# Three key parts in memory, maxima ahead of operand loads, a leaner beginning and values in whole blocks, in a gated cross-attention kernel on Trainium2

## The chip, the cores and the metric

One core of a Trainium2 chip runs the kernel. It has five engines with their own instruction streams: TensorE (PE, matmuls and transposes into PSUM), ScalarE (ACT, activations), VectorE (DVE, reductions and elementwise work), GpSimd (POOL, elementwise work in SBUF) and SyncE (SP, which issues the transfers). They are ordered only by semaphores. The metric is the device time of one execution in microseconds (us).

## The reference

A batch of 16 sequences of 256 tokens with 128 features attends to 16 contexts of up to 1601 rows, with 16 heads of depth 8, and then passes through a mixture of 8 small experts. All in float32; the softmax runs over all 1601 keys.

```python
# attention: q from layernorm(x), k and v from ctx_1024
qh, kh, vh = split(layernorm(x) @ wq.T + bq), split(ctx @ wk.T + bk), split(ctx @ wv.T + bv)
attn = softmax(einsum('bhqd,bhkd->bhqk', qh, kh) / sqrt(8), axis=-1)
x = x + tanh(g_xattn[0]) * (einsum('bhqk,bhkd->bhqd', attn, vh) @ dense_w.T + dense_b)
# experts, on layernorm(x): sigmoid gates, the two best of 8, their weights normalised
h = gelu(x_n @ W1[e] + b1[e]);  y[e] = h @ W2[e] + b2[e]
x = x + tanh(g_ffn[0]) * (sum_e gate[e] * y[e] + gelu(x_n @ Ws1 + bs1) @ Ws2 + bs2)
```

## The kernel before

The 16 heads are 8 pairs of heads. One step `s` handles one batch `b = s // 2` and one half of its pairs (`GP = 4`), for all 256 queries and all 1601 keys, in 13 tiles of up to 128 keys; there are 32 steps. Four steps are one phase cycle, called a pass below: `PLAN` has one string for each step of it.

Scores are computed with the float32 operands split into three bfloat16 parts. A contraction over 48 rows holds six products of parts (`KPART`, `QPART`), each for the 8 features of a head; the two heads of a pair lie on two sides of the partitions (`SIDE`). Keys are split by `split_run` (DVE, batch 0) or `split_keys` (POOL, the others, four operations), stored to memory by `store_keys` (line 389) and loaded in the operand's layout by `load_operands` (line 318). `PLACES` says which parts are repeated: the first part of the keys stands in three places of the contraction, the second in two, the third in one. In the kernel before all six places are written to memory: `k_dram` has six slots, stored by three DMAs for each of two halves.

The softmax subtracts a maximum per query and head. `row_scores` (PE, line 741, called a row score below) computes scores of 128 queries against 512 keys for both heads of a pair, `maximum` (DVE, line 901) reduces them; 24 such and 2 for the rest of 65 keys make one step. `neg_max` is transposed on PE (unit `T`, line 697), copied by ACT (605), split in three by POOL (`split_maxima`), and `move_maxima` (SP, line 410) writes the parts to `m_dram` (416) and reads them back as three more rows of the query operand (419). So the score matmul already gives score minus maximum.

`score_pair` (PE, line 757, a pair below) computes keys against queries for four units in two of the three PSUM banks `a_ps`; ACT takes the exponential of each bank (573) into `probs`. `values` (PE, line 775) multiplies the probabilities of a tile of 128 keys with the values, four matmuls side by side in the array, summed in `o_ps`. A block is one such tile of one step; it can be done whole (512 columns, letter pair `VV` in `PLAN`) or in two halves of 256 columns (two `V` apart). The same three banks also serve, in order, the key projection of the next batches (`K`, line 688), the value projection (`V`, 692), the transposes of maxima and the second layer's tiles. Row scores, the dense projection and the second layer's outputs use two other slots, `b_ps`.

PE works in the order that `order(s)` writes out from `PLAN`: `P` a pair, `S` a row score (for the step after next or next), `V` values, `k` and `v` projections, `T` the transpose of the maxima of the next step, `d` the dense projection, `q` and `f` the query tiles and the second layer, `y` and `c` its output. `S` runs ahead of `P`: in step `s` the row scores of step `s + 1` are completed before `T`, and ten of step `s + 2` follow. ACT and DVE follow the same order for their parts.

SP issues all transfers in one stream. In step `s` it takes, in this order: outputs of the last step (`move_outputs`), in odd steps the keys two batches on (`store_keys`), the operands of step `s + 3` (`load_operands`), the reciprocal sums and the gates, in odd steps the two contexts (`load_context`), the maxima of step `s + 1` (`move_maxima`), the queries of the next chunk and the result. Each call first waits for what it needs, and all behind it wait too. Before step 0 SP loads the first context, weights, constants, all tokens and the value context, stores the first keys and queries, and loads the first operands.

## Time and profile before

| | us |
|---|---|
| time, median of 3 runs | 1434.74 (1431.17 to 1438.01) |
| the profiled execution | 1436.73 |
| its span, from the first to the last instruction | 1434.9 |
| PE busy | 1241.7 (87%) |
| ACT busy | 1055.6 (74%) |
| DVE busy | 1049.3 (73%) |
| POOL busy | 418.7 (29%) |
| mean granted clock of TensorE | 0.902 of full speed |
| bytes moved by DMA | 147.13 MB |

Busy time is the sum of an engine's instructions. A matmul that runs beside another counts in the same busy time, and a busy PE need not be at its peak: at a granted clock of 0.5 (1.2 GHz) the same matmuls are busy for longer than at 1.0 (2.4 GHz). A time in square brackets in a timeline row is the idle time of the engine just before, and the arrow names what ended it.

### The profile page before, as it was taken

To read this page: it belongs to the slowest core of one execution; us is meant where nothing else is said; L and a number is where in the kernel's file an instruction comes from. 1 tells how busy PE (TensorE), PEld (TensorE's weight loads), DVE (VectorE), ACT (ScalarE), POOL (GpSimd) and SP (SyncE) were. 2 spreads that over 40 slices of the span, in tenths; PEclk is the share of its full clock that TensorE was granted. 3 is DMA by queue.
4 is the path that set the end of the run, shared out by engine and by line. 5 is a ranking of instruction groups with operands and counts; after the bars stand their busy time and mean duration, and the time that the engine had idled before them with its cause. 6 is when DMAs were issued, how large, how long until landed. Compare 5 with 4: busy or idle time off the path is not lost.

```text
span 1434.9 us, 29778 instructions
## 1 busy us (share of the span) xinstructions
PE 1241.7 (87%) x11555; PEld 458.9 (32%) x11555; DVE 1049.3 (73%) x1208; ACT 1055.6 (74%) x1962; POOL 418.7 (29%) x309
## 2 busy tenths in 40 slices
PE   2448889798989999899989999799979999799855
PEld 1112323232323433243323333243323433243224
DVE  8477778587768888688868878688768868689001
ACT  1008879587978799688968789688968889689741
POOL 7242224051333215151424125051423205010111
PEclk6568999798988999899989999899989999899786
DMA  7673634636273653737273744637173744501101
GB/s 213 114 149 69 150 70 98 140 84 129 53 164 70 139 119 87 147 81 149 52 169 61 170 87 99 139 82 146 47 167 67 165 92 96 102 11 33 31 14 45
DMA packets 71390, 147.13 MB, mean 103 GB/s; under 512 B 13705, under 2 KB 37970, under 8 KB 71250
## 3 DMA queue, kind: packets, MB, share of 16 engines
q1 hardware_dynamic: 71250, 145.24, 47.4%
q8 instruction: 91, 1.49, 0.5%
q14 instruction: 49, 0.40, 0.1%
HBM read 88.30 MB, written 56.91 MB: 101 GB/s over the span
## 4 chain that ended last, share of the span: by engine, by line
PE 66%; DMA 14%; ACT 5%; DVE 4%; SPq 4%; POOL 3%; issue 2%; POOLq 0%; ACTq 0%; DVEq 0%
PE o_ps L775 26%; PE a_ps L757 15%; PE b_ps L741 11%; DMA m_dram<-nm_parts 10%; PE a_ps L688 4%; PE a_ps L692 4%; ACT probs L573 3%; PE b_ps L720 2%; DVE run_max L901 2%; SPq L406 2%; DMA q_op<-m_dram 1%; SPq L397 1%; PE a_ps L684 1%; PE b_ps L723 1%; DMA q_op<-q_dram 1%
## 5 line engine op out<-in xcount | busy, mean ns | idle before, releaser
L901 DVE TENSOR_REDUCE run_max<-b_ps 128x2 f32<-128x1024 f32 x768 | 899.4, 1218 | 249.4 <-PE b_ps L741 246.0
L573 ACT ACTIVATE probs<-a_ps 128x512 f32<-128x512 f32 (+1 forms) x1664 | 901.9, 594 | 144.3 <-PE a_ps L757 127.4
L775 PE MATMUL o_ps<-probs,v_op 128*32 128x256 f32 (+3 forms) x4928 | 505.8, 483 | 2.3 <-ACT probs L573 1.2
L757 PE MATMUL a_ps<-q_op,k_op 51*128 51x256 bf16 (+1 forms) x3328 | 338.1, 283 | 46.4 <-DMA q_op<-m_dram 25.6
L741 PE MATMUL b_ps<-k_op,q_op 48*128 48x512 bf16 (+1 forms) x2048 | 325.6, 350 | 37.5 <-DVE run_max L901 24.2
L757 PEld LDWEIGHTS a_ps<-q_op,k_op 51*128 51x128 bf16 (+1 forms) x3328 | 112.9, 97 | 373.5 <-ACT probs L573 307.3
L741 PEld LDWEIGHTS b_ps<-k_op,q_op 48*128 48x128 bf16 x2048 | 88.7, 96 | 208.2 <-DVE run_max L901 95.9
L775 PEld LDWEIGHTS o_ps<-probs,v_op 128*32 128x32 f32 (+1 forms) x4928 | 98.4, 109 | 176.4 <-issue 93.8
L509 POOL TENSOR_TENSOR attn<-num,den_all 128x256 f32<-128x256 f32 x16 | 11.6, 728 | 440.3 <-DMA den_all<-r_dram 440.3
L688 PE MATMUL a_ps<-kctx,wk_s 128*128 128x400 f32 (+1 forms) x128 | 81.4, 734 | 55.7 <-DMA kctx<-ctx_t 49.9
L469 POOL TENSOR_TENSOR nm_parts<-nm_t,one 8x256 bf16<-8x256 f32 x32 | 19.3, 602 | 360.5 <-ACT nm_t L605 360.5
L594 ACT ACTIVATE k_t<-a_ps,bk_s 128x401 f32<-128x401 f32 (+1 forms) x64 | 38.1, 597 | 106.7 <-PE a_ps L688 106.6
L692 PE MATMUL a_ps<-wv_s,vctx 128*128 128x128 f32 (+1 forms) x416 | 64.4, 294 | 0.0
L888 DVE SCALAR_TENSOR_TENSOR y_s<-b_ps,tgf,x_s 128x128 f32<-128x128 f32 x32 | 11.2, 349 | 71.3 <-PE b_ps L724 71.2
L599 ACT ACTIVATE v_op<-a_ps 128x512 f32<-128x512 f32 x64 | 32.9, 513 | 36.7 <-PE a_ps L692 36.3
L692 PEld LDWEIGHTS a_ps<-wv_s,vctx 128*128 128x128 f32 (+1 forms) x416 | 51.2, 192 | 20.8 <-issue 11.5
L469 POOL TENSOR_TENSOR k_parts<-k_t,one 128x1601 bf16<-128x1601 f32 x15 | 42.8, 2850 | 43.8 <-ACT k_t L594 43.8
L688 PEld LDWEIGHTS a_ps<-kctx,wk_s 128*128 128x128 f32 x128 | 25.9, 248 | 83.1 <-issue 61.0
L904 DVE TENSOR_REDUCE run_max<-b_ps 128x8 f32<-128x520 f32 x64 | 43.9, 696 | 10.3 <-PE b_ps L741 10.3
L471 POOL TENSOR_TENSOR k_t<-k_t,k_parts 128x1601 f32<-128x1601 f32 x15 | 48.5, 3230 | 1.2
L475 POOL TENSOR_TENSOR k_parts<-k_t,k_parts 128x1601 bf16<-128x1601 f32 x15 | 45.3, 3021 | 1.2
L473 POOL TENSOR_TENSOR k_parts<-k_t,one 128x1601 bf16<-128x1601 f32 x15 | 42.8, 2851 | 1.2
(100 smaller groups left out, 680.4 us busy)
## 6 DMA issues: line engine op xcount, KB each, us to landing
k_op<-k_dram SPq DMA_DIRECT2D x64, 600.4 KB, 9.5
k_dram<-k_parts SPq DMA_DIRECT2D x32, 600.4 KB, 6.0
kctx<-ctx_t SPq DMA_DIRECT2D x16, 800.5 KB, 12.5
vctx<-ctx_t SPq DMA_DIRECT2D x16, 800.5 KB, 11.8
k_dram<-k_parts SPq DMA_DIRECT2D x32, 400.2 KB, 7.0
o_dram<-o_s SPq DMA_DIRECT2D x32, 256.0 KB, 2.1
g_all<-g_dram SPq DMA_DIRECT2D x16, 512.0 KB, 6.4
k_dram<-k_parts SPq DMA_DIRECT2D x32, 200.1 KB, 6.7
```

What stands on the lines that cost most here:

```text
L469: pool.tensor_tensor(parts[0], whole, ones(whole, slice(0, whole.shape[0])), ALU.mult).then_inc(chain, 1)
L471: pool.tensor_tensor(whole, whole, parts[0], ALU.subtract).then_inc(chain, 1)
L473: pool.tensor_tensor(parts[1], whole, ones(whole, slice(0, whole.shape[0])), ALU.mult).then_inc(chain, 1)
L475: pool.tensor_tensor(parts[2], whole, parts[1], ALU.subtract).then_inc(chain, 1)
L573: act.activation(probs[0:keys, unit % PB, :], a_ps[at % AB][0:keys, :], ACT.Exp, scale=SCALE).then_inc(a_taken, 1)
L688: last = pe.matmul(bank[:, 0:n_keys], wk_s[:, :], kctx[:, k0:k0 + n_keys], start=True, stop=True)
L692: last = pe.matmul(bank[0:KEYS[t], 128 * (t % 4):128 * (t % 4) + 128], vctx[:, 128 * t:128 * t + KEYS[t]], wv_s[:, :], start=True, stop=True)
L741: last = pe.matmul(slot[:, side, to:to + n_keys], q_op[buf][rows, p, 128 * t:128 * t + 128], k_op[buf][rows, p, k0:k0 + n_keys], start=Tru ...
L757: last = pe.matmul(a_ps[(at + side) % AB][0:KEYS[t], SEQ * a:SEQ * a + SEQ], k_op[buf][rows, slot, 128 * t:128 * t + KEYS[t]], q_op[buf][r ...
L775: last = pe.matmul(o_ps[32 * j:32 * j + 32, cols], v_op[s // 2 % 2][0:KEYS[t], t, GP * (s % 2) + j, :], probs[0:KEYS[t], unit % PB, cols], ...
L901: dve.tensor_reduce(run_max[:, t, :, p, c:c + 1].rearrange("q v o -> q (v o)"), slot[:, :, :], AX.X, ALU.max).then_inc(b_taken, 1)
L904: dve.tensor_reduce(run_max[:, i - FULL, :, :, RUNS], slot[:, :, 0:GP * REST].rearrange("q v (p k) -> q v p k", p=GP), AX.X, ALU.max).then ...
```

## The change

- **Three key parts.** `k_dram` holds each of the three parts once. `store_keys` issues two DMAs instead of six; `load_operands` issues three for the key operand of each side instead of one, each reading the first parts from memory again, so 8 DMAs a step instead of 4.
- **Order of SP.** In odd steps `move_maxima(s + 1)` stands ahead of `load_operands(s + 3)` and of the value context. The key context of batch `b + 3` is loaded in the even step, after the maxima, not in the odd one.
- **The beginning.** The first operands are loaded right after the first keys are stored; the queries of chunk 0 are stored from ACT's queue; only the tokens of chunk 0 are loaded ahead of them, those of chunk 1, the operands of step 1, the value context and the other tokens behind. DVE waits for the tokens where it first needs them. `first_maxima` reorders steps -2 and -1: five row scores before the key tiles, and all row scores and the transpose of step 0 ahead of the rest.
- **PLAN.** Four new strings. They hold the same numbers of `P`, `S`, `V`, `k`, `T`, `f`, `q` and `d`; every `V` now stands beside another, so that all blocks are whole. The four outputs of a chunk (`y`, `c`) are all in the second string.

```diff
-OP_DMAS = 4
+OP_DMAS = 2 * (len(PLACES) + 1)
-PART_STORES = 2 * len(PLACES)
+PART_STORES = 2
 PLAN = (
-    "SkSPVVPSkSPSkSPVVPSVPSVPSVPSVPSVPSVPSVPVSPyPSVVSPcSPVVPSSTkSPVVPSVPSVPSVPSVPdSPVVPVVPS",
-    "vSPSVVSPvSPVVSPyPcSPVVPSVVSPyPSfcPSVVPSfSPVVSPVVSPyPcSPVVSPSvPVVPSSTvVPSVPSVPSVPSVPVSPSVPVS",
-    "PVPSVPSkVPVSPSVPVPSVPSVPSfSPVVPSkSPVVPSVPSVPSVPSVSPVSPVSPSVVPSffffTfSPSVVvSPSkSPVVPSkSPVVP",
-    "dSPvSPSVVSPvSPVVPSVPSVPSVPSvVPSVPSVPSVPSVPSVPSVPSqSSPVVPqSPVVTPSVPSVPSVPSVPSVPSVPSVVP",
+    "PSkSPVVSPSvPSVVPSSPVVPSSPVVPkSSPVVPSkSPVVPSSPVVPSSPVVPSSPVVTSPSVVPdPSSPVVPVVPSkSPVVPS",
+    "yPcSPVVSSPvSPVVPSSPVVPSSPVVPSvSPSVVPVVSPyPcSPVVPSVVvPSSfSPVVPSTyPcSPVVSPSVVPyPcSPVVSPSVVPSfS",
+    "PSPVVPkSPVVPVVPkSPSkPVVPSSPVVPSfSPVVPSSPVVPSSPVVPSSPVVPSSPVVTPSSPVVPSkSPVVSPSfffffSSPVVS",
+    "vSPVVPSvSPSvPVVPSSPVVPSqSPVVPSSPVVPSSPVVPSSPVVPVVPdPSSvSPVVTSPSqPSVVPSSPVVPSSPVVPSSPVV",
 )
+def first_maxima():
+
+    scores = [event for event in ORDER[-2] if event[0] == "S"]
+    rest = [event for event in ORDER[-2] if event[0] != "S"]
+    first = [event for event in ORDER[-1] if event[0] == "S" and event[1] < SUNITS]
+    turn = [("A", ("T", 0, 0))]
+    return scores[:5] + rest + scores[5:], first + turn + [e for e in ORDER[-1] if e not in first + turn]
+
+
+ORDER[-2], ORDER[-1] = first_maxima()
...
-                    sp.dma_start(k_op[buf][rows, :, :].rearrange("r (a p) c -> r a p c", a=2),
-                                 kd[:, :, pairs, :]).then_inc(op_in[buf], 16)
+                    for r0, r1 in PLACES:
+                        to = slice(SIDE * side + DH * r0, SIDE * side + DH * r1)
+                        sp.dma_start(k_op[buf][to, :, :].rearrange("r (a p) c -> r a p c", a=2),
+                                     kd[0:DH * (r1 - r0), :, pairs, :]).then_inc(op_in[buf], 16)
...
-                    for r0, r1 in PLACES:
-                        sp.dma_start(k_dram[b % 2, a, r0:r1].rearrange("n r c -> r n c"),
-                                     k_parts[64 * a:64 * a + 64, 0:r1 - r0, :]).then_inc(k_written, 16)
+                    sp.dma_start(k_dram[b % 2, a].rearrange("n r c -> r n c"),
+                                 k_parts[64 * a:64 * a + 64, :, :]).then_inc(k_written, 16)
...
+            store_keys(0)
+            load_operands(0)
+            load_context("K", kctx, 1, kctx_in)
+            load_tokens(1, 2, x_in[1])
+            load_operands(1)
             load(vctx, ctx_t[0]).then_inc(vctx_in, 16)
-            store_keys(0)
-            load_context("K", kctx, 1, kctx_in)
-            store_queries(0)
-            load_operands(0)
+            load_tokens(2, CHUNKS, x_in[2])
             for s in range(FIRST, LAST + 1):
                 b = s // 2
                 if 0 <= s - 1 < STEPS:
                     move_outputs(s - 1)
                 if s % 2 == 1 and b + 2 < BATCH:
                     store_keys(b + 2)
-                if 0 <= s + 3 < STEPS:
+                if s % 2 == 0 and 2 <= s + 3 < STEPS:
                     load_operands(s + 3)
                 if s % 2 == 0 and 0 <= b - 1 < BATCH:
                     spread_sums(b - 1)
                 if s % 4 == 2 and 0 <= (s - 6) // 4 < CHUNKS:
                     spread_gates((s - 6) // 4)
-                if s % 2 == 1 and b + 3 < BATCH:
+                if 0 <= s + 1 < STEPS:
+                    move_maxima(s + 1)
+                if s % 2 == 1 and 2 <= s + 3 < STEPS:
+                    load_operands(s + 3)
+                if s % 2 == 0 and b + 3 < BATCH:
                     load_context("K", kctx, b + 3, kctx_in)
                 if s % 2 == 1 and 0 <= b + 2 < BATCH:
                     load_context("V", vctx, b + 2, vctx_in)
-                if 0 <= s + 1 < STEPS:
-                    move_maxima(s + 1)
...
# ACT, after the first units:
+            store_queries(act, 0)
# DVE, before statistics("q", (s + 6) // 4):
+                            if s < 4:
+                                dve.wait_ge(x_in[s // 4 + 2], 16 if s < 0 else 16 * (CHUNKS - 2))
```

## Rows read from the trace of the kernel before

**Rows 1.** Windows: stretch, length, busy (instructions) of PE, PEld, DVE, ACT, POOL, clock, DMA share, GB/s
```profile
426.00:587.30 161.30, 153.74 (x1448) 56.92 (x1446) 129.19 (x148) 132.09 (x246) 51.71 (x38) 0.93 0.52 112
```
**Rows 2.** Waits of PE, 110 to 1378 us: total, times, longest
```profile
PE a_ps L688 <- DMA kctx<-ctx_t: 36.7, 6, 7.7
PE a_ps L757 <- DMA q_op<-m_dram: 25.6, 15, 7.2
```
**Rows 3.** Timeline, 571 to 598 us: start, duration, engine, line, operation
```profile
571.86 0.33 SPq L332 DMA_DIRECT2D k_op<-k_dram  x1
...
575.44 0.29 SPq L416 DMA_DIRECT2D m_dram<-nm_parts  x1
...
585.35 1.68 PE L688 MATMUL a_ps<-kctx,wk_s 128*128 128x401 f32 x2 [4.40 <-DMA kctx<-ctx_t]
...
587.33 0.58 SPq L419 DMA_DIRECT2D q_op<-m_dram  x2
...
589.13 0.61 PE L757 MATMUL a_ps<-q_op,k_op 51*128 51x256 bf16 x4 [1.57 <-DMA q_op<-m_dram]
...
597.43 0.38 PE L757 MATMUL a_ps<-q_op,k_op 51*128 51x256 bf16 x4
```
**Rows 4.** Windows: the beginning, a wait, a lesser dip, a stretch without row scores
```profile
0.00:54.00 54.00, 12.04 (x21) 5.21 (x21) 29.73 (x34) 6.21 (x11) 25.85 (x17) 0.63 0.81 197
...
587.00:599.00 12.00, 10.43 (x53) 2.72 (x52) 6.04 (x5) 6.60 (x12) 0.00 (x0) 0.57 0.35 90
...
1146.80:1185.50 38.70, 36.24 (x319) 12.13 (x320) 25.63 (x25) 31.96 (x57) 3.26 (x5) 0.91 0.43 86
...
1355.00:1366.00 11.00, 9.35 (x116) 2.62 (x116) 0.00 (x0) 10.71 (x21) 0.00 (x0) 1.00 0.01 5
```
**Rows 5.** Timeline: maxima with an empty queue, and pairs with a whole block
```profile
137.06 0.27 SPq L416 DMA_DIRECT2D m_dram<-nm_parts  x1
138.43 0.56 SPq L419 DMA_DIRECT2D q_op<-m_dram  x2
...
1367.07 0.39 PE L757 MATMUL a_ps<-q_op,k_op 51*128 51x256 bf16 x4
...
1368.15 0.39 PE L757 MATMUL a_ps<-q_op,k_op 51*128 51x256 bf16 x4 [0.69 <-ACT probs L573]
...
1368.47 1.06 PE L775 MATMUL o_ps<-probs,v_op 128*32 128x512 f32 x8
...
1369.47 0.39 PE L757 MATMUL a_ps<-q_op,k_op 51*128 51x256 bf16 x4
...
1369.90 7.56 ACT L573 ACTIVATE probs<-a_ps 128x512 f32<-128x512 f32 x14 [0.23 <-PE a_ps L757]
```
**Rows 6.** Timeline: a key tile, and pairs with half blocks
```profile
65.78 0.94 PE L688 MATMUL a_ps<-kctx,wk_s 128*128 128x400 f32 x2
...
572.75 8.01 DVE L901 TENSOR_REDUCE run_max<-b_ps 128x2 f32<-128x1024 f32 x7 [0.84 <-PE b_ps L741]
...
573.21 0.39 PE L757 MATMUL a_ps<-q_op,k_op 51*128 51x256 bf16 x4
573.44 0.38 PE L741 MATMUL b_ps<-k_op,q_op 48*128 48x512 bf16 x2
...
574.32 0.39 PE L757 MATMUL a_ps<-q_op,k_op 51*128 51x256 bf16 x4
```
**Rows 7.** Timeline and chain of waits, the beginning
```profile
32.60 8.12 SPq L406 DMA_DIRECT2D q_dram<-q_parts  x12
54.16 1.03 PE L741 MATMUL b_ps<-k_op,q_op 48*128 48x512 bf16 x4 [12.48 <-DMA q_op<-q_dram]
...
96.17 12.79 DMA m_dram<-nm_parts
...
110.81 0.61 PE L757 MATMUL a_ps<-q_op,k_op 51*128 51x256 bf16 x4 [1.52 <-DMA q_op<-m_dram]
```
**Rows 8.** Key stores: issue time in ns, min/median/max
```profile
L397 SPq DMA_DIRECT2D k_dram<-k_parts x96: 581/1384/2912, 21.0 to 1208.9; - x96
```
**Rows 9.** Value matmuls by shape (eight to a block or half block)
```profile
L775 PE MATMUL o_ps<-probs,v_op 128*32 128x256 f32 x3072 | 250.5, 398 | 0.9 <-ACT o_s L581 0.4
```

More of the change, by code:

```diff
@@ L264, in flamingo_block @@
         y_s = sb("y_s", [128, 4, 128])
-        key_in, first_in, const_in, x0_in, x_in, ones_set = (sem(n) for n in ("key_in", "first_in", "const_in", "x0_in",
-                                                                              "x_in", "ones_set"))
+        key_in, first_in, const_in, ones_set = (sem(n) for n in ("key_in", "first_in", "const_in", "ones_set"))
+        x_in = [sem(f"x_in{i}") for i in range(3)]
         k_ones, v_ones = [sem(f"k_ones{i}") for i in range(4)], sem("v_ones")
@@ L297, in keys_split, with store_queries @@
                 engine.wait_ge(k_chain, 4 * b)
+        def store_queries(engine, c):
+            engine.wait_ge(q_chain, 4 * (c + 1))
+            for a in range(2):
+                for part, (r0, r1) in enumerate(PLACES):
+                    for r in range(r0, r1):
+                        engine.dma_start(q_dram[2 * c:2 * c + 2, a, r].rearrange("b r q -> r b q"),
+                                         q_parts[64 * a:64 * a + 64, part, :]
+                                         .rearrange("p (b q) -> p b q", b=2)).then_inc(q_written, 16)
         block = ctx.enter_context(nc.Block())
@@ L309, in _, with load_tokens @@
                 load(dst, src).then_inc(key_in, 16)
-            sp.dma_start(x_s[:, 0:4, :], x[:, 0:4, :]).then_inc(x0_in, 16)
+            def load_tokens(c0, c1, arrived):
+                for c in range(c0, c1):
+                    sp.dma_start(x_s[:, 4 * c:4 * c + 4, :], x[:, 4 * c:4 * c + 4, :]).then_inc(arrived, 16)
+            load_tokens(0, 1, x_in[0])
             for dst, src in firsts:
@@ L314, in _ @@
                 load(dst, src).then_inc(const_in, 16)
-            for c in range(1, CHUNKS):
-                sp.dma_start(x_s[:, 4 * c:4 * c + 4, :], x[:, 4 * c:4 * c + 4, :]).then_inc(x_in, 16)
             def load_operands(s):
@@ L395, in store_keys @@
                 for a in range(2):
-                    for r0, r1 in PLACES:
-                        sp.dma_start(k_dram[b % 2, a, r0:r1].rearrange("n r c -> r n c"),
-                                     k_parts[64 * a:64 * a + 64, 0:r1 - r0, :]).then_inc(k_written, 16)
-            def store_queries(c):
-                sp.wait_ge(q_chain, 4 * (c + 1))
-                for a in range(2):
-                    for part, (r0, r1) in enumerate(PLACES):
-                        for r in range(r0, r1):
-                            sp.dma_start(q_dram[2 * c:2 * c + 2, a, r].rearrange("b r q -> r b q"),
-                                         q_parts[64 * a:64 * a + 64, part, :]
-                                         .rearrange("p (b q) -> p b q", b=2)).then_inc(q_written, 16)
+                    sp.dma_start(k_dram[b % 2, a].rearrange("n r c -> r n c"),
+                                 k_parts[64 * a:64 * a + 64, :, :]).then_inc(k_written, 16)
             def move_maxima(s):
@@ L442, in _ @@
                     load_context("V", vctx, b + 2, vctx_in)
-                if 0 <= s + 1 < STEPS:
-                    move_maxima(s + 1)
                 if s % 4 == 3 and 0 < (s + 5) // 4 < CHUNKS:
-                    store_queries((s + 5) // 4)
+                    store_queries(sp, (s + 5) // 4)
                 if s % 4 == 1 and 0 <= (s - 9) // 4 < CHUNKS:
@@ L934, in _ @@
             dve.memset(k_op[0][:, :, :], 1.0).then_inc(k_ones[0], 1)
-            dve.wait_ge(x0_in, 16)
+            dve.wait_ge(x_in[0], 16)
             statistics("q", 0)
```

4 lines of the change are left out of this document (2 added, 2 removed).

## Prediction

> **What bounds the kernel now.** After the page's busy shares I read windows of four steps each. Such a pass (two batches of keys, one chunk of the second layer) is the unit that repeats; the five in the middle take 158 to 164 us, 162 in the mean, of which TensorE (PE) is busy 154, ScalarE (ACT) 132, VectorE (DVE) 129 in the one shown [rows 1]: three engines near each other, none full. Next, who waits: between the first score tile and the last, PE stands 36.7 us for a context transfer in 6 places and 25.6 us for the maxima rows in 15 [rows 2]. The reader is to see in the SyncE (SP) timeline how one place comes about: SP queues the operands of a later step, then two contexts, and only then the maxima of the next step; that tiny write, issued at 575.44, is followed by its dependent issue at 587.33, and the context for the keys lands so late that PE waits 4.40 us, then 1.57 us more [rows 3]. The granted clock is 0.57 in the 12 us around it and 1.00 in a stretch without such a wait [rows 4]; between 589.13 and 597.43 the matmuls run at 1.2 GHz. And the start: the first score tile runs at 110.81 us [rows 7].
>
> The profiled execution took 1436.73 us (span 1434.9), 2.0 above the median of the runs, 1434.74. I take differences from the trace and subtract them from the median.
>
> **Part 1, key parts and issues.** Per batch the stores fall from six DMAs (12 parts of 64 x 1601 x 2 bytes, 2401 KB) to two (6 parts, 1201 KB); their issue, 1.38 us each at the median [rows 8], falls from 8.3 to 2.8 us. The operand loads carry the same bytes in eight instead of four DMAs, each under 0.5 us of SP [rows 3]: under +2 us per step. Both lie beside compute; SP's next need in an odd step is the maxima, some 10 us later. Cost 0, bounds -1 to +2 us per step pair only if SP were late, which nothing in [rows 3] suggests after the reorder.
>
> **Part 2, maxima and contexts.** In odd steps the maxima go ahead of the next operand load and the value context; the key context moves to the step before and so lands some 30 us early. With nothing ahead of it the write takes 1.4 us from issue to dependent issue [rows 5] instead of 11.9. Gone: 36.7 us, and 24 of the 25.6 (1.5 belongs to the beginning), 61 together. With them goes what the low clock costs. From 589.13 to 597.43 PE did three score pairs, one whole value block, four row scores and two key tiles; at full clock a pair takes PE 0.31, a block 1.00, a row score 0.23, a key tile 0.94 [rows 5, 6]; that is 4.7 us, not 8.3, and the key tile before it took 0.7 more than it would: 4.3 us a place. Seven places (six contexts, one maxima wait of 7.2 us): 30. Five lesser dips in the second halves of passes, as one with a mean clock of 0.91 over 38.7 us [rows 4]: some 7 us at 1.2 GHz each, 35 together, 0.4 us lost per us as above, less the waits in them: 8. Sum -99, bounds -61 (clock falls for other reasons) to -110.
>
> What is queued behind the moved step matters. Behind the maxima now stand eight operand DMAs and then the value context. In the last step of a pass the new order puts the transpose of the maxima some eight score pairs before the end, and the next batch's first value tile after only three pairs of the new pass (before: late in the step before or at leisure). From the transpose: 0.7 us to ACT's end, 2.6 us of POOL (four splits of 0.60 to 0.66), write and rows, then eight issues: the context is issued about 9.3 us later. The queue moved 2994 KB from 571.86 to 587.33 [rows 3], 193 KB/us; 1393 + 800 KB from 5.7 us on end at 17.2. PE asks at 4 x 2.40 + 0.6 + 4 = 14.5. **New wait: 2.7 us**, eight times: +21. Bounds: 0 (if PE arrives later) to 5 us and a low clock, (5 + 4.3) x 8 = +74.
>
> **Part 3, values in whole blocks.** Before, 3072/8 = 384 half blocks and 216 whole ones [rows 9]; after, by counting the letters of the order, 416 whole. Halves run pair, row score, half, in 1.11 us, with no idle on PE; DVE needs 8.01/7 = 1.144, so two cost 2.29 [rows 6]. A whole block takes 1.00 on PE against 2 x 0.57 (1.11 less a pair and a row score, 0.54), but it stands between score pairs: 1367.07 to 1369.47 is pair, pair, block in 2.40 us, and ACT idles 0.23 in it [rows 5]. The three banks hold only one pair ahead. So a bare block costs 0.11 more; where another tile is in it, the 0.32 us that PE has free pays for it. Per pass, new: 52 x 2.40 = 124.8, plus what the tiles add beyond the slack (keys 8 x 0.55, values 4.8, second-layer outputs 4 x 1.2, hidden tiles with two table loads 6.5, all others 3.7) = 149.0. Old: 25 x 2.29 + 27 x 2.08 (two pairs, two row scores, a block) + the same tiles at full PE time 34.2 (keys 7.5, values 7.3, outputs 6.1, hidden 6.5, others 6.8) = 147.6; the traced pass less its stalls, 162 - 99/8 = 149.6, agrees within 2. **+1.4 a pass, +11 in all.** Bounds: PE's chain alone, 104 x 0.54 + 52 + 34.2 = 142.4 a pass (-42), and no slack used, 124.8 + 34.2 = 159 (+91); I take the value between, being the one that reproduces the old pass. In the last 36 pairs there are no row scores; ACT paces halves at 7.56/7 = 1.08 a pair [rows 5], blocks at 1.20: +4.
>
> **Part 4, the beginning.** Before: six key stores, key context, twelve query stores from 32.60 for 8.12 us, operands, first row scores 54.16 [rows 7]. The DMA engines are 0.81 busy at 197 GB/s [rows 4]: bytes, not latencies. After: nothing but constants ahead, stores 1.2 MB from 21, query stores on ACT beside them (0.8 MB from 21.9 on; twelve issues at SP's 0.68 end at 30.1), landed by 32.3; 1.4 MB of operands, issued in 3.4 us, landed near 43. The maxima of step 0 then take 26 x 1.14, statistics 1.4 and a wait of up to 2 for the second token chunk: 75. Before, the transpose waited behind the query tiles and the write took 12.79 us [rows 7]; now the rows are there at about 82. The ten row scores of step 1 (11.4 us of DVE) still stand ahead of the first pair, so it runs at 86, not 110.8. **-25**, bounds -12 (only the transfer chain shortens) to -32. The later token chunks, 1.5 MB, now share the queue with steps -1 and 0; their wait (before step 2) is 40 us away.
>
> One rule of the Trainium skill bears on this ("DMA: Bandwidth & Descriptors", section "Issuing engines are not separate DMA queues"): moving the query stores to ACT saves issue time only, as all queues share the same 16 engines. Had I granted the move no more than issue time, the start would gain the 8 us of issues and little from overlap, and the sum would stand some 5 us higher.
>
> **Sum**: 1434.7 - 25 - 99 + 21 + 11 + 4 = **1347 us**. The tail (57 us after the last pair) I cost at nothing: its output tiles fill the same wait for normalisation.
>
> **Rivals.**
> A. *PE-bound whole blocks.* The saved 0.14 us a block counts in full wherever other tiles lie and PE is the one without idle, as in the half-block stretch of [rows 6]. At 142.4 a pass, 6.6 less than I take: 1347 - 53 = 1294. Against: the 2.40 is measured.
> B. *The value context becomes the new place that drops the clock.* 5 us and 4.3 us eight times instead of 2.7: +53, 1400. For: same queue, same 2.2 MB as now. Against: maxima waits of 1 to 3 us in the middle left the windows at 1.00.
> C. *The beginning or the low clock gives little back* (ACT's stores slow, clock falls anyway): 1347 + 25 = 1372 or more.
> D. *Slower than before.* The new order sets two row scores side by side ahead of a pair. There are two slots in memory for them and DVE takes 1.14 us each, 2.29 of every 2.40; with its gates, statistics and divisions DVE is saturated, and a row score that waits holds the in-order PE and so the pair and ACT. The second is due 0.45 us after the first pair, which leaves 0.4 us until the banks would hold the pair anyway; from a wait of 0.61 us a block on (0.21 lost x 416 = 88) the gains are gone; at 0.7 us the time is 1347 + 125 = 1472. For: seven maxima in a row run without a gap now [rows 6]. Against: DVE is busy 129 of 161 us [rows 1], 129 of about 153 after.
> E. *The clock.* With 0.3 us idle in each block the clock could fall often. The rows speak against it: 1355 to 1366, pairs and halves alone with PE 85% busy, was granted 1.00 [rows 4], and pair, pair, block ran at its speed [rows 5]. A quarter of the steady stretch at 1.2 GHz would cost 0.4 x 300 = 120: 1467.
> The Trainium skill has that as a rule ("TensorE: Matmul & The Clock Gate", section "A second HAM failure mode: psum-queue depth-cycling"): short idles between groups of matmuls can make the clock oscillate. By that rule, E's 1467; the rows of this trace speak against it.
>
> **Chances.** Forecast 0.49 (its own range 1318 to 1375), A 0.17, B 0.13, C 0.11, D 0.06, E 0.04. Range for 8 in 10: 1295 to 1405, which takes in A's middle and B's. A measurement of this kernel tells 0.5% (7 us) from no change. Faster 0.87, same 0.04, slower 0.09: D and E almost whole, B and C with bad luck both.
>
> **What would show it.** First score tile near 86 us, first row scores near 43. No PE wait on the key context after it; maxima waits under 3 us in all; write to dependent issue about 1.4 us in odd steps. A wait of value tiles for their context, once a pass, under 4 us. Granted clock above 0.95 in the steady windows. 3328 value matmuls, block to block 2.40 us where nothing else is in it, a pass near 153 us. I am wrong if a pass is above 159 or below 145, or if ACT's idle for score tiles grows beyond DVE's.

## The result and the profile after

The changed kernel takes 1476.67 us (median of four, 1470.38 to 1490.08), the kernel before 1432.95 beside it (1426.57 to 1438.01): 1.032 times the time, 95% interval 1.024 to 1.040. It is slower by some 44 us where 88 less were forecast; 1477 lies outside the range. The profiled execution took 1470.38 us, its span is 1468.6. Below, medians are of all executions of a kernel and ratios of the undisturbed ones; the one execution of e4 that was traced took 2629.38 us against 1447 to 1456 of its three others, and nothing is read from it.

First the waits of PE, by line, tile and releaser (total, times, longest):

```profile
PE a_ps L713 <- DMA vctx<-ctx_t: 73.6, 8, 10.9
PE a_ps L778 <- ACT probs L593: 43.9, 113, 1.4
PE b_ps L762 <- DVE run_max L921: 35.0, 45, 6.4
```

The waits for the key context are gone and those for the maxima rows have shrunk to 5.1 us, as forecast against [rows 2]. But a wait that is not among those of [rows 2] now stands at the value tiles, 73.6 us in eight places where 21 were forecast. The window that answers to [rows 1]:

```profile
424.00:585.00 161.00, 144.94 (x1242) 51.77 (x1240) 128.25 (x149) 131.41 (x245) 51.23 (x38) 0.97 0.51 96
```

PE is busy 9 us less than before in a pass of the same length, at a higher granted clock (0.97 for 0.93). What it works less it stands longer. The six passes from 256 to 1245 us take 165 us in the mean, 162 in the middle of the kernel before, 153 forecast; by its own sign, a pass above 159, the prediction is wrong.

One of the eight places, from the timeline (start, duration, engine, line; idle time before it in brackets), and then the one long piece of the chain of waits:

```profile
418.92 0.38 PE L718 MATMUL a_ps<-ident,neg_max 128*8 128x128 f32 x2
422.58 0.30 SPq L432 DMA_DIRECT2D m_dram<-nm_parts  x1
423.98 0.57 SPq L435 DMA_DIRECT2D q_op<-m_dram  x2
424.66 1.06 SPq L359 DMA_DIRECT2D k_op<-k_dram  x3
426.11 1.89 SPq L359 DMA_DIRECT2D k_op<-k_dram  x3
428.39 0.47 SPq L414 DMA_DIRECT2D vctx<-ctx_t  x1
439.74 0.54 SPq L370 DMA_DIRECT2D o_dram<-o_s  x1
443.37 2.04 PE L713 MATMUL a_ps<-wv_s,vctx 128*128 128x128 f32 x8 [9.78 <-DMA vctx<-ctx_t]
```
```profile
428.39 14.85 DMA vctx<-ctx_t
```

The mechanism is the forecast's: maxima out at once (1.40 us from write to dependent issue, against 11.89 in [rows 3]), eight operand DMAs, then the context, issued 9.5 us after the transpose (forecast 9.3). PE asked 14.7 us after it (443.37 - 9.78 - 418.92; forecast 14.5). Only the transfer is off: from the first operand issue to the context's landing 18.6 us pass, not 11.5. The 2.19 MB moved at 118 KB/us, not 193. Twelve stores of queries (768 KB) are issued right behind the context in such a place (from 428.90), and could be thought the cause. They are not: between 180 and 760 us the context lands 14.8 to 16.2 us after its issue in the four places with them and 14.3 to 17.5 us in the four without.

What lowers that rate shows in windows of an undisturbed operand load (stretch, length, busy of PE, PEld, DVE, ACT and POOL, clock, DMA share, GB/s), issued from 438.75 in the kernel before and from 448.10 in the kernel after; the first row is of contexts, later in the queue of an odd step before:

```profile
421.00:424.00 3.00, 0.00 (x0) 0.00 (x0) 0.00 (x0) 0.00 (x0) 0.00 (x0) 0.87 0.96 341
...
441.00:444.00 3.00, 3.00 (x42) 1.06 (x42) 2.86 (x4) 2.95 (x6) 0.00 (x0) 1.00 1.06 167
444.00:447.00 3.00, 3.00 (x42) 0.94 (x38) 3.00 (x3) 2.92 (x7) 0.00 (x0) 1.00 1.10 188
447.00:450.00 3.00, 3.00 (x43) 1.55 (x36) 2.45 (x3) 2.84 (x7) 0.00 (x0) 1.00 0.53 62
```
```profile
450.00:453.00 3.00, 2.92 (x25) 0.92 (x26) 2.96 (x4) 2.53 (x6) 0.00 (x0) 1.00 1.15 130
453.00:456.00 3.00, 3.00 (x25) 0.84 (x24) 2.24 (x3) 2.71 (x6) 0.00 (x0) 1.00 0.94 117
456.00:459.00 3.00, 2.96 (x30) 0.97 (x30) 2.69 (x4) 2.76 (x6) 0.00 (x0) 1.00 0.81 121
459.00:462.00 3.00, 2.34 (x30) 0.79 (x30) 2.49 (x4) 2.76 (x6) 0.00 (x0) 1.00 0.56 60
```

The share is the mean busy share of the 16 DMA engines. Before, they work on the load together and stop nearly together: in windows of 1 us the share is 0.70 from 448 and 0.09 from 449, 10.4 us after the first issue. After, at the same bytes, the share falls in steps, 1.15, 0.94, 0.81, 0.56, is still 0.40 from 462 and 0.05 from 463, 14.9 us after the first issue. A mean share near a half in the last microseconds fits engines of which some have finished while others go on. The eleven loads of this kind from 150 to 1050 us agree: in windows of 0.5 us they end 10.5 to 12.0 us after their first issue before (median 11), and 13.5 to 15.5 after (median 15). A small write that stands behind, the reciprocal sums, is followed by its dependent issue 6.7 us later before (443.79 to 450.49) and 11.1 after (453.22 to 464.31).

The beginning, timeline of the kernel after, answers to [rows 7]:

```profile
51.36 1.04 PE L762 MATMUL b_ps<-k_op,q_op 48*128 48x512 bf16 x4 [17.04 <-DMA q_op<-q_dram]
58.83 0.87 DVE L847 BATCH_NORM_STATS2 stats_q<-x_s 128x6 f32<-128x128 f32 x4 [4.39 <-DMA x_s<-x]
62.05 5.71 PE L709 MATMUL a_ps<-kctx,wk_s 128*128 128x401 f32 x8
91.42 0.58 PE L718 MATMUL a_ps<-ident,neg_max 128*8 128x128 f32 x2 [1.15 <-DVE neg_max L931]
97.30 10.27 DVE L921 TENSOR_REDUCE run_max<-b_ps 128x2 f32<-128x1024 f32 x9 [6.03 <-PE b_ps L762]
106.90 0.63 PE L778 MATMUL a_ps<-q_op,k_op 51*128 51x256 bf16 x4
```

### The profile page after: what moved, and what is told of

It reads as the page before. It is cut to its first block, busy times and chain, and to the rows that moved or that the text cites. A ratio compares the mean times of both kernels' runs of the same rounds, so it can differ in the third digit from the quotient of the medians.

```text
span 1468.6 us, 26642 instructions
## 1 busy us (share of the span) xinstructions
PE 1219.8 (83%) x9955; PEld 429.9 (29%) x9955; DVE 1057.0 (72%) x1208; ACT 1057.9 (72%) x1962; POOL 418.7 (29%) x309
## 3 DMA queue, kind: packets, MB, share of 16 engines
HBM read 88.30 MB, written 37.24 MB: 85 GB/s over the span
## 4 chain that ended last, share of the span: by engine, by line
PE 53%; DMA 21%; DVE 12%; ACT 5%; issue 3%; POOL 3%; SPq 2%; ACTq 1%; POOLq 0%; DVEq 0%
PE o_ps L796 21%; PE a_ps L778 13%; DVE run_max L921 10%; DMA vctx<-ctx_t 8%; PE b_ps L762 7%; DMA r_dram<-den 6%; ACT probs L593 4%; PE a_ps L713 4%; PE a_ps L709 2%; PE b_ps L741 2%; DMA x_s<-x 1%; DMA den_all<-r_dram 1%; DMA m_dram<-nm_parts 1%; DMA o_dram<-o_s 1%; SPq L359 1%
## 5 line engine op out<-in xcount | busy, mean ns | idle before, releaser
L796 PE MATMUL o_ps<-probs,v_op 128*32 128x512 f32 (+1 forms) x3328 | 461.8, 628 | 0.2 <-ACT probs L593 0.2
L762 PE MATMUL b_ps<-k_op,q_op 48*128 48x512 bf16 (+1 forms) x2048 | 309.2, 346 | 59.1 <-DVE run_max L921 35.0
L713 PE MATMUL a_ps<-wv_s,vctx 128*128 128x128 f32 (+1 forms) x416 | 71.8, 320 | 73.6 <-DMA vctx<-ctx_t 73.6
L489 POOL TENSOR_TENSOR nm_parts<-nm_t,one 8x256 bf16<-8x256 f32 x32 | 19.3, 604 | 269.0 <-ACT nm_t L625 269.0
L796 PEld LDWEIGHTS o_ps<-probs,v_op 128*32 128x32 f32 (+1 forms) x3328 | 66.5, 109 | 99.3 <-issue 69.6
L713 PEld LDWEIGHTS a_ps<-wv_s,vctx 128*128 128x128 f32 (+1 forms) x416 | 58.7, 217 | 94.8 <-issue 80.4
L709 PE MATMUL a_ps<-kctx,wk_s 128*128 128x400 f32 (+1 forms) x128 | 67.2, 620 | 5.6 <-DMA bk_s<-bk 5.6
L899 DVE SCALAR_TENSOR_TENSOR x_s<-b_ps,tgx,x_s 128x256 f32<-128x256 f32 x16 | 7.7, 484 | 65.1 <-PE b_ps L730 64.7
L489 POOL TENSOR_TENSOR k_parts<-k_t,one 128x1601 bf16<-128x1601 f32 x15 | 42.8, 2852 | 34.5 <-ACT k_t L614 34.5
L924 DVE TENSOR_REDUCE run_max<-b_ps 128x8 f32<-128x520 f32 x64 | 43.2, 696 | 12.5 <-PE b_ps L762 12.5
L535 POOL TENSOR_TENSOR hid<-hid,g_all 128x2048 f32<-128x2048 f32 x8 | 36.2, 4529 | 28.5 <-DMA g_all<-g_dram 20.4
## 6 DMA issues: line engine op xcount, KB each, us to landing
vctx<-ctx_t SPq DMA_DIRECT2D x16, 800.5 KB, 16.2
```

What stands on the lines that cost most here:

```text
L489: pool.tensor_tensor(parts[0], whole, ones(whole, slice(0, whole.shape[0])), ALU.mult).then_inc(chain, 1)
L709: last = pe.matmul(bank[:, 0:n_keys], wk_s[:, :], kctx[:, k0:k0 + n_keys], start=True, stop=True)
L713: last = pe.matmul(bank[0:KEYS[t], 128 * (t % 4):128 * (t % 4) + 128], vctx[:, 128 * t:128 * t + KEYS[t]], wv_s[:, :], start=True, stop=True)
L762: last = pe.matmul(slot[:, side, to:to + n_keys], q_op[buf][rows, p, 128 * t:128 * t + 128], k_op[buf][rows, p, k0:k0 + n_keys], start=Tru ...
L796: last = pe.matmul(o_ps[32 * j:32 * j + 32, cols], v_op[s // 2 % 2][0:KEYS[t], t, GP * (s % 2) + j, :], probs[0:KEYS[t], unit % PB, cols], ...
L924: dve.tensor_reduce(run_max[:, i - FULL, :, :, RUNS], slot[:, :, 0:GP * REST].rearrange("q v (p k) -> q v p k", p=GP), AX.X, ALU.max).then ...
```

## The experiments

Each is one kernel against the kernel before on the same chip (medians of 1430 to 1434 us). The ratio is that of the run to it, with its 95% interval.

**1 to 4: which part?**

e1, in odd steps the value context ahead of the operand load:
```diff
-                if s % 2 == 1 and 2 <= s + 3 < STEPS:
-                    load_operands(s + 3)
                 if s % 2 == 1 and 0 <= b + 2 < BATCH:
                     load_context("V", vctx, b + 2, vctx_in)
+                if s % 2 == 1 and 2 <= s + 3 < STEPS:
+                    load_operands(s + 3)
```


> The changed kernel, but in odd steps SP issues the value context ahead of the operand load, right behind the maxima. Theory (queue): the 73.6 us that TensorE waits for the value context in 8 places, 9.2 each, are the price of its place behind 1393 KB of operands; issued about 6 us after the transpose of the maxima instead of 9.5, and with nothing ahead, it lands some 5 us later, before the 14.6 us at which TensorE asks. The waits go, and with them 4.3 us of low clock in each place: 1477 - 74 - 34 = about 1370 us; a pass of four steps takes about 151 us instead of 165. Rival (whole blocks): the passes are long because of the 2.40 us that a block of two pairs takes, and the wait only stands where ScalarE would idle anyway: 1440 us or more, with ScalarE's idle for score tiles grown. Rival (something behind it): the operands, now later, are waited for: then a wait of row scores on the operand load appears.

1455.80 us, ratio 1.018 (1.014 to 1.022). PE's wait for the context is gone, but only 21 of the 107 us that the theory gave for it. The rival band (1440 or more) holds the number, not for its reason. In place of PE's wait DVE waits, 19.3 us of it in the tail, where the changed kernel waits as long (total, times, longest):
```profile
DVE den L952 <- DMA num<-o_dram: 80.1, 9, 19.3
```
The outputs of the step (line 376 of the changed kernel) now stand behind the moved load. DVE works in order, so row scores, and PE behind them, wait for `num`: PE's wait for `run_max` grew from 35.0 to 81.4 us.

e2, the same operand built from loads of 16 rows: the places of the parts are permuted, so that each of the three DMAs of a side reads two parts.
```diff
-KPART = [0, 1, 2, 0, 1, 0]
-QPART = [0, 0, 0, 1, 1, 2]
-PLACES = [(0, 3), (3, 5), (5, 6)]
+KPART = [1, 0, 1, 0, 0, 2]      # parts lie in memory in the order 1, 0, 2
+QPART = [0, 0, 1, 1, 2, 0]
+PLACES = [(0, 2), (2, 4), (4, 6)]
+SOURCE = [0, 0, 1]              # first part read, for each place
```


> The changed kernel with the places of the contraction in another order, so that the three key loads of a side take 16 rows each instead of 24, 16 and 8: as many DMAs, as many bytes, parts read from memory as often. Theory (split of rows): the operand load takes about 14 us alone because a DMA of 24 or 8 rows is spread over fewer of the 16 engines; with 16 rows it comes back to the 11 to 12 us it had with one DMA of 48 rows; the value wait falls from 9.2 to about 6 us a pass, the first row scores start at about 48 us instead of 51.4: 1477 - 26 - 4 = about 1447 us. Rival (repeated reads, or more DMAs): the load is slower since the same part is read three times, or for the count of DMAs; then nothing changes, 1477 us, and the waits stay at 9.2. (The Trainium skill, page DMA: Bandwidth & Descriptors, section Why a DMA increments its semaphore by 16 and not by 1, says that a DMA uses the largest number of engines up to 16 that divides its outermost dimension; that would be 12, 16 and 8 here.)

1412.82, ratio 0.990 (0.985 to 0.994): 64 us less than the changed kernel with the same bytes and the same number of DMAs, twice what was expected. The context's median landing falls from 16.2 to 11.5 us (11.8 before). The windows of its operand load, issued from 423.80:
```profile
426.00:429.00 3.00, 2.92 (x32) 0.70 (x24) 2.96 (x3) 2.77 (x6) 0.00 (x0) 1.00 0.90 112
429.00:432.00 3.00, 3.00 (x26) 0.95 (x24) 2.24 (x4) 2.68 (x6) 0.00 (x0) 1.00 1.14 136
432.00:435.00 3.00, 3.00 (x28) 0.95 (x24) 3.00 (x3) 2.71 (x5) 0.00 (x0) 1.00 0.97 114
435.00:438.00 3.00, 2.52 (x40) 0.88 (x34) 2.22 (x4) 2.60 (x5) 0.00 (x0) 1.00 0.28 26
```
The long fall of the share is gone: in windows of 1 us it is 0.81 from 435 and 0.02 from 436, 12.2 us after the first issue. The eleven loads end after 11.5 to 12.5 us (median 12), against 15 in the changed kernel and 11 before. But while all engines are busy the rate, 112 to 136 GB/s, is no higher than in the changed kernel. So the uneven rows account for 3 of the 4 us by which the load became longer; the other 1 comes with the eight DMAs or the repeated reads, which is not shown.

e3, the changed kernel with the four old strings of `PLAN`:
```diff
-PLAN = (new strings)
+PLAN = (strings of the kernel before)
```


> The changed kernel with the order strings of the kernel before (400 half blocks, value tiles where they stood before). Theory (queue): the first value tile of a batch then stands a step later or late in a step, so that the value context has landed: no wait for it, none for the key context (it is still loaded a step earlier), none for the maxima. A pass is 162 - 12.4 = about 150 us, the total about 1477 - 8 x 15 = 1355 us. Rival (the transfers are the cause): operands in eight DMAs are too slow whatever the order; waits of TensorE on DMA stay over 50 us and the time over 1430. Rival (whole blocks are worth it): then the time is above that of the kernel with the values' context first.

1488.67, ratio 1.042 (1.037 to 1.047). A miss, as 1355 was expected; the intervals of this kernel and the changed one (1.024 to 1.040) overlap. Whole blocks are not what cost the time. DVE waits 131.5 us for `num` in 15 places.

e4, the kernel before with only the new strings, the reverse edit:

> The kernel before with the new order strings alone: six key slots in memory, old order of SP, old beginning. Theory: the key context still comes late (loaded in the odd step behind the operands), and the first value tile now stands early in a pass, with its context queued last of all ahead of the maxima; TensorE waits 8 to 10 us for one of them once a pass and for the maxima in the odd steps: a pass of 165 to 170 us, total 1460 to 1500 us, and block to block 2.40 us. Rival: the strings alone bring the gain or the loss; if the waits on DMA are no more than the 62 us of before, the difference from 1433 is the cost of whole blocks, which I had put at +11 us (bounds -42 and +91).

1455.82, ratio 1.017 (1.011 to 1.022), a little under the lower end. Without a trace of such an execution, where its 25 us go stays open.

**5 to 8: rows of a DMA, or number of DMAs and slots?**

e5 is e2 with the swap of e1:

> Rows of 16 and, in odd steps, the value context ahead of the operand load. Theory 1 (with loads of 16 rows the queue has room): the 46.6 us that PE still waited for the value context and the clock lost with them go, and the outputs, which came late behind slow operand loads in the first run with this swap (DVE waited 80 us for num), are not late now: 1413 - 46 = 1367, 1355 to 1380; DVE waits for num under 30 us. Theory 2 (the queue is full in any order): the outputs come late again, DVE waits 60 us or more for num, and the time stays at 1405 to 1425.

1402.42, ratio 0.979 (0.973 to 0.986), 3 us under the band of theory 2 and 22 above that of theory 1: DVE waits 59.0 us for `num` in eight places, 19.3 of it in the tail.

e6 is e2 with the old strings:

> Rows of 16 with the order strings of before. Theory 1 (the slow loads alone made the old order bad in the run with it, 1488.7): DVE's wait for num goes from 131.5 us to under 30, and by the forecast's own terms for the order (+11, +4 and +21 for the new one) this gives 1413 - 36 = 1377, 1360 to 1395. Theory 2 (the new strings are worth something by themselves once the queue is arranged as it is now): 1420 to 1440.

1431.59, ratio 1.000 (0.995 to 1.005), in the band of theory 2. DVE waits 90.1 us for `num` in 15 places. Loads of 16 rows do not cure that; something else delays the outputs.

e7, part 1 undone alone in the changed kernel:
```diff
-OP_DMAS = 2 * (len(PLACES) + 1)
-PART_STORES = 2
+OP_DMAS = 4
+PART_STORES = 2 * len(PLACES)
...
-                    for r0, r1 in PLACES:
-                        to = slice(SIDE * side + DH * r0, SIDE * side + DH * r1)
-                        sp.dma_start(k_op[buf][to, :, :]...
+                    sp.dma_start(k_op[buf][rows, :, :]...
```


> The changed kernel with part 1 undone alone: six slots in memory, stored by six DMAs, each side's keys loaded by one DMA of 48 rows. Theory 1 (loads of 24, 16 and 8 rows are what costs, not how much is stored): within 12 us of the run with rows of 16 (1413), 1401 to 1425. Theory 2 (three slots save traffic that counts): 1430 or more, since the stores are 1201 KB a batch more. Theory 3 (the split is innocent, rows of 16 helped for another reason): near 1470.

1408.86, ratio 0.985 (0.979 to 0.991), as e2. Three slots in place of six save nothing that counts; for the kernel's time the 48 rows in one DMA are as good as three times 16, though an operand load ends after 10.5 to 11.0 us here (eleven loads, median 11).

e8, the kernel before with only the split:
```diff
-                    sp.dma_start(k_op[buf][rows, :, :].rearrange("r (a p) c -> r a p c", a=2),
-                                 kd[:, :, pairs, :]).then_inc(op_in[buf], 16)
+                    for r0, r1 in PLACES:
+                        to = slice(SIDE * side + DH * r0, SIDE * side + DH * r1)
+                        sp.dma_start(k_op[buf][to, :, :].rearrange("r (a p) c -> r a p c", a=2),
+                                     kd[DH * r0:DH * r1, :, pairs, :]).then_inc(op_in[buf], 16)
```


> The kernel before with only its operand loads split: each side's keys by three DMAs of 24, 16 and 8 rows from the same six slots, the same bytes, eight DMAs a step in place of four. Theory 1 (a DMA whose rows do not divide over all 16 engines loads some of them more): waits for maxima, contexts and outputs grow, 1460 to 1490. Theory 2 (the split costs only together with the new order of SP): 1430 to 1440.

1524.52, ratio 1.067 (1.059 to 1.076): the split alone costs 91 us, more than the top of the expectation. The two waits of [rows 2] grow, over the whole span from 49.9 and 25.6 us to:
```profile
PE a_ps L690 <- DMA kctx<-ctx_t: 87.6, 8, 13.2
PE a_ps L759 <- DMA q_op<-m_dram: 61.8, 15, 11.4
```
This kernel reads each of the six slots once, as the kernel before, and its operand loads still end only after 12.5 to 15.0 us (median 14.5): reading one part several times is not the main cause.

**9 to 12: the order of SP and the beginning.**

e9 is e5 with the sums and gates of even steps ahead of the operand load:
```diff
-                if s % 2 == 0 and 2 <= s + 3 < STEPS:
-                    load_operands(s + 3)
                 if s % 2 == 0 and 0 <= b - 1 < BATCH:
                     spread_sums(b - 1)
                 if s % 4 == 2 and 0 <= (s - 6) // 4 < CHUNKS:
                     spread_gates((s - 6) // 4)
+                if s % 2 == 0 and 2 <= s + 3 < STEPS:
+                    load_operands(s + 3)
```


> Rows of 16, in odd steps the value context ahead of the operand load, and in even steps the sums and gates ahead of the operand load. Theory 1 (what is left is that small transfers stand in a queue behind operand loads, and DVE and PE wait in order behind them): the 40 us that DVE still waited for num within the steps fall under 15, the write of the sums is followed by its dependent issue in under 3 us instead of some 7 to 10, and the time goes from 1402 to 1375 to 1390. Theory 2 (DVE's wait for num comes from operand loads of the odd step before, which this does not move): 1395 to 1405, with num waits near 40 us.

1413.53, ratio 0.985 (0.981 to 0.990): 11 us more than e5, though the intervals overlap, where 12 to 27 less were expected of theory 1. The sums go out at once (median landing 1.4 us), but DVE's wait for `num` stays (59.7 us) and SP's wait for the maxima write grows from about 50 us in the changed kernel to 94.8.

e10 is e2 with e9's edit and the odd operand load back in its old place:
```diff
                 if s % 2 == 1 and b + 2 < BATCH:
                     store_keys(b + 2)
+                if s % 2 == 1 and 2 <= s + 3 < STEPS:
+                    load_operands(s + 3)
...
                 if 0 <= s + 1 < STEPS:
                     move_maxima(s + 1)
-                if s % 2 == 1 and 2 <= s + 3 < STEPS:
-                    load_operands(s + 3)
```


> Rows of 16, sums first in even steps, and in odd steps the operand load back in its place right after the key stores, with only the contexts behind the maxima. Theory 1 (the outputs come late because the operand load was moved to stand directly ahead of them): DVE's wait for num within the steps falls to near 0, PE's wait for the value context too, and maxima waits stay under 6 us since the load is done by then: 1375 to 1390. Theory 2 (in its old place the load delays the maxima as before): PE waits 15 us or more for maxima rows, 1400 or more.

1361.12, ratio 0.949 (0.945 to 0.954): better than expected. `num` is waited for 23.3 us, of which 19.4 is the tail's; PE waits 8.7 us for maxima rows; no value-context wait is left among the large ones.

e11, of the changes only the beginning (e7 with the old strings and, in the steps, the old order of SP):

> Of the changes only the beginning, with six slots in memory, loads of 48 rows, the old order of SP in the steps and the old order strings. Theory 1 (the step of the forecast): -25 with bounds -12 to -32, so 1401 to 1421 against 1433. Theory 2 (the first pair comes earlier, but the low clock of the beginning lasts and the steps behind take back the gain): within 7 us of 1433.

1432.90, ratio 0.999 (0.996 to 1.003). Theory 2. In its timeline the first row scores are 3 us earlier (51.10 against 54.16), less than the 8.12 us of issues that SP no longer has ahead of them. The first pair is 3.6 us later (114.38 against 110.81): step -1 still queues operands and contexts ahead of the maxima.
```profile
51.10 1.04 PE L759 MATMUL b_ps<-k_op,q_op 48*128 48x512 bf16 x4 [22.62 <-DMA q_op<-q_dram]
99.47 0.68 SPq L431 DMA_DIRECT2D m_dram<-nm_parts  x1
112.57 0.58 SPq L434 DMA_DIRECT2D q_op<-m_dram  x2
114.38 0.61 PE L775 MATMUL a_ps<-q_op,k_op 51*128 51x256 bf16 x4 [1.56 <-DMA q_op<-m_dram]
```

e12, the kernel before with only the new order of SP in the steps (the loop as in the diff, old beginning, old strings, 48 rows):

> The kernel before with only the new order of SP in the steps: maxima ahead of the operand load and the value context in odd steps, key context in the even step. Loads of 48 rows, old strings, old beginning. Theory 1 (the forecast's step, without the new value-context wait, as the old strings ask for values later): -99 with bounds -61 to -110, 1323 to 1372. Theory 2 (the moved operand load now stands ahead of the outputs, and DVE waits for num and holds the row scores): waits for contexts and maxima are gone from PE, DVE waits 80 us or more for num, 1415 to 1440.

1401.38, ratio 0.976 (0.970 to 0.981): 31 us of gain, about half of the step's least (61) and outside the bands of both theories. PE's waits for contexts and maxima are gone from its list but for one of 5.5 us at the beginning, and its first pair runs at 100.95. What took the gain is in SP's and DVE's waits and in one piece of its chain of waits:
```profile
SPq L349 <- DMA o_dram<-o_s: 132.1, 32, 10.5
```
```profile
DVE den L934 <- DMA num<-o_dram: 67.5, 15, 9.7
```
```profile
490.27 9.41 DMA o_dram<-o_s
```
A write of 256 KB that landed 2.0 to 4.5 us after its issue before (SP waited 57.2 us in 32 places) takes up to 10.9 behind the moved load.

**13 to 16: do the two causes add up, and what are whole blocks worth?**

e13 is the changed kernel with the one edit of e10 on the odd operand load (rows of 24, 16 and 8):

> The changed kernel (rows of 24, 16 and 8) with one edit: in odd steps the operand load right after the key stores, only the contexts behind the maxima. Theory 1 (split and place each cost, and add up): the 1361 of the run with both mended plus some 60 for the split, 1410 to 1435. Theory 2 (the place alone made the slow loads costly): within 15 us of 1361.

1401.37, ratio 0.977 (0.973 to 0.982): 9 us below the band of theory 1 and 25 above that of theory 2, so nearer to adding up. What the rows still cost here is in part another wait, 17.3 us in the same kernel with rows of 16 (e14 below):
```profile
PE b_ps L730 <- POOL attn L529: 32.1, 8, 12.4
```
`attn` needs the reciprocal sums, a write of 16 KB that is issued behind the operand load of the even step. The first pair is 8.3 us later as well (106.6 against 98.3). That is some 23 of the 40 us by which the two kernels differ; the rest was not followed.

e14 is e2 with the same edit, sums in their old place:

> Rows of 16 and the operand load early, as in the run of 1361, but in even steps the sums behind the operand load again. Theory 1 (sums first gave nothing and cost some maxima waits): 1350 to 1361. Theory 2 (sums first was part of the gain): 1370 to 1390.

1361.75, ratio 0.948 (0.944 to 0.952), at the upper edge of theory 1; sums first had no part in e10's gain that can be measured. The waits of PE, and two passes:
```profile
PE a_ps L779 <- ACT probs L594: 40.9, 103, 1.4
PE b_ps L763 <- DVE run_max L922: 26.8, 46, 1.9
```
```profile
420.66:572.71 152.05, 147.19 (x1252) 51.37 (x1244) 129.23 (x149) 132.01 (x247) 51.82 (x39) 0.98 0.53 102
572.71:723.40 150.69, 144.88 (x1256) 51.15 (x1248) 130.13 (x150) 133.21 (x248) 51.80 (x38) 1.00 0.52 103
```

e15, the kernel before with one edit, the maxima ahead of the contexts alone:
```diff
-                if s % 2 == 1 and b + 3 < BATCH:
+                if 0 <= s + 1 < STEPS:
+                    move_maxima(s + 1)
+                if s % 2 == 0 and b + 3 < BATCH:
                     load_context("K", kctx, b + 3, kctx_in)
                 if s % 2 == 1 and 0 <= b + 2 < BATCH:
                     load_context("V", vctx, b + 2, vctx_in)
-                if 0 <= s + 1 < STEPS:
-                    move_maxima(s + 1)
```


> The kernel before with one edit: the maxima ahead of both contexts, the key context in the even step; the operand load keeps its place ahead of the maxima. Theory 1 (the contexts alone delayed the maxima, and with the load early no output comes late): better than the run that moved the load too (1401), 1370 to 1390. Theory 2 (the load also delays the maxima): PE waits 20 us or more for maxima rows, 1400 to 1415.

1378.68, ratio 0.960 (0.955 to 0.964). The smaller move gains 56 us, theory 1, where the one that takes the load along gains 31. Its price is a wait of 34.4 us for maxima rows in eight places.

e16 is e14 with the old strings:

> Rows of 16 and the operand load early, with the order strings of before. Theory 1 (whole blocks cost time by themselves, 15 us by the forecast's terms): 10 to 15 us below the same kernel with the new strings. Theory 2 (the new strings are worth something): 15 to 25 us above it.

1353.03, ratio 0.941 (0.935 to 0.946), the lowest of all, 9 us under e14. The intervals overlap, so the two are not told apart.

The four kernels with the new strings and the new beginning lie in a square:

| us | load behind the maxima | load right after the key stores |
|---|---|---|
| rows of 24, 16, 8 | 1476.7 (the changed kernel) | 1401.4 (e13) |
| rows of 16 | 1412.8 (e2) | 1361.8 (e14) |

Each mend is worth more where the other is missing: the split costs 64 and 40, the place 75 and 51 us. Together they are 115.

## Why the prediction was wrong

**The step that failed first is part 1**: "The operand loads carry the same bytes in eight instead of four DMAs", cost 0. I priced the issue of the DMAs and their bytes and took it that any DMA spreads alike. e8 puts 91 us on this one edit; in the changed kernel it is 64 (e2). The cause is how the rows are split, not the number of DMAs (e2 has eight as well), nor the slots (e7) or the repeated reads (e8). The rows of a DMA and the partition at which it begins changed together (0, 24, 40 against 0, 16, 32), and no run tells the two apart. The windows above fit engines that run dry one after the other. That is what the Trainium skill says ("DMA: Bandwidth & Descriptors", section "Why a DMA increments its semaphore by 16 and not by 1"): a DMA uses the largest number of engines, at most 16, that divides both sides' outermost dimension, and these are the lowest-numbered. Of 24, 16 and 8 rows that makes 12, 16 and 8 engines; as an estimate from this, the first eight hold 4 rows each (2 + 1 + 1) where an even spread of 48 rows over 16 gives 3, 1.33 times an even share. By the medians the load of the changed kernel took 15 us, 1.25 times the 12 of e2 with as many DMAs and 1.36 times the 11 of the kernel before: the estimate lies between, so the traces agree. No run here shows the single engines.

**The second step that failed is part 2's 193 KB/us**, a mean over a stretch that held two contexts. The windows around the operand loads show 167 and 188 GB/s with 48 rows in one DMA, 117 to 130 with 24, 16 and 8, and 112 to 136 with three times 16; contexts were moved at 341 in the kernel before. So a part of the low rate stays when the rows are even. The bound that I gave for the new wait, 5 us a place, was exceeded: 9.2 in the mean (73.6 in 8). This is rival B's mechanism at twice its price; I gave it 0.13 and worked out 1400. That D (1472) and E (1467) name numbers close to the measured one is chance: their mechanisms did not occur, as the next paragraphs say.

**The third is what the prediction did not look at.** It named the value context as queued behind the moved load, but not the outputs of the same step, which come next. In [rows 3] the load stood far ahead of them; moved behind the maxima, it stands directly before. e1, e3, e5, e6, e9 and e12 all show DVE waiting for `num` in its place, with the row scores and PE in order behind it. Whoever comes first behind the load pays: the context in the changed kernel (DVE waits 25.0 us for `num`, 19.3 of it in the tail), the outputs when the context is put ahead. The place is worth 51 us even with good rows, and moving the contexts alone (e15) already takes more than moving both (e12).

**What held.** The order of events around the maxima, to 0.2 us. The cadence of the whole block: 407.51, 409.91 and 412.31 in the timeline of the changed kernel are two periods of 2.40 us, so neither D nor A. Nor E: the granted clock is 0.98 and 1.00 in the two passes of e14, which have the same blocks and not the wait. In the six passes of the changed kernel it is 0.93 to 0.97, and in the place shown it is 1.00 from 431 to 434 and 0.50 from 437, after PE has come to stand. The pass without the new wait, 150.3 by the forecast (153 less 2.7), is 152.05 and 150.69 in e14. The sign of whole blocks (+15) is not contradicted in the best arrangement (+9, not told apart), but with the load behind the maxima the new strings are faster, by 19 us with rows of 16 (e6) and by 12, not told apart, with the split (e3): the old ones have DVE wait for `num` in 15 places there. How the strings bring that about was not tried. The 384 half blocks of part 3 leave out those on the rest of 65 keys; the letters give 400, and the sum per pass uses that count (25).

**Part 4 was mis-sized.** The first pair runs at 106.9, not 86. Of these 21 us about 8 come from the operands (51.4 for 43, the same rate error; 47.6 with rows of 16), 2.4 from the wait for the second token chunk (4.4, which I had bounded by 2), and 4.5 where DVE waited for key tiles, which stood between the row scores and ran at a granted clock of 0.51 (5.71 us for eight matmuls). The rest, some 6, lies behind the transpose, where PE does the first value tiles and DVE stands 6.03 us before its next row score. With rows of 16 the first pair runs at 98.2. e11 shows that the beginning alone is worth nothing, since the order of SP holds the maxima up, and e12 that the order alone takes the first pair to 100.95, 9.9 of the 12.6 us that it gains in e2: what I booked there belongs mostly to part 2.

So 1477 - 1347 = 130 us are: 64 for the rows, 51 for the place of the load (taken in this order), 15 left, for most of which the first pair would account, 12 us later than forecast even with rows of 16. In another order of the two mends the first two shares would be 40 and 75.

## What to carry to other kernels

Price a DMA also by how its rows divide over the engines, not by bytes and issues alone; here rows of 48 and 16 were good and 24, 16 and 8 were not, and permuting what the rows mean was enough to get there. When a large transfer is moved in a queue, list the next small transfers behind it until the first that an in-order engine waits for; what they pay comes off the gain of the move. Give way to the small and urgent by moving as little as possible: putting only the contexts last gained 56 us, taking the load along 31.

## What was not expected of the hardware

Eight DMAs a step with rows of 16 cost the kernel nothing that can be measured against four with 48 (1412.82 and 1408.86), though the load itself takes some 12 us against 11, while eight with 24, 16 and 8 cost 40 to 91 us. Writing 19.67 MB less to memory (56.91 to 37.24 MB) moved nothing that can be measured. The same DMA engines, all busy, gave 167 to 188 GB/s on operand loads and 341 on a context, so a rate is taken from the row of the transfer that is priced.
